# Counting products of the rank passes: four column tiles, in the middle of an LSTM step

## The reference

```python
def step(carry, x_t):
    h_prev, c_prev = carry
    combined = jnp.concatenate((x_t, h_prev), axis=1)
    f_t = jax.nn.sigmoid(combined @ W_f + b_f)
    i_t = jax.nn.sigmoid(combined @ W_i + b_i)
    c_tilde = jnp.tanh(combined @ W_c + b_c)
    c_t = f_t * c_prev + i_t * c_tilde
    o_t = jax.nn.sigmoid(combined @ W_o + b_o)
    h_t = o_t * jnp.tanh(c_t)
    return ((h_t, c_t), h_t)
_, hs = jax.lax.scan(step, (h0, c0), jnp.swapaxes(x, 0, 1))
```

## Time and profile before

| | |
|---|---|
| median of 3 runs | 4644.66 us (4644.18 to 4644.81) |
| the profiled execution's own time | 4646.08 us |
| its span, first to last instruction | 4644.3 us |
| mean granted TensorE clock | 0.971 |
| TensorE matmuls busy | 4446.2 us (96%) |
| VectorE busy | 2307.4 us (50%) |
| ScalarE busy | 1912.3 us (41%) |
| matmuls of line 1007 (the adds), busy | 2310.0 us |
| matmuls of line 1063 (the counting products) | 640 |

### The profile page before, as it was taken

One profiled execution on the slowest core, in us unless ns is written; L12 is line 12 of the kernel. 1 busy time (PEld: TensorE's weight loads), 2 busy tenths in 40 slices (PEclk: granted clock), 3 DMA queues, 4 the chain that ended last, 5 costly groups with the idle time before them and its releaser, 6 DMA issues.

```text
span 4644.3 us, 136942 instructions
## 1 busy us (share of the span) xinstructions
PE 4446.2 (96%) x53052; PEld 2196.5 (47%) x53052; DVE 2307.4 (50%) x10628; ACT 1912.3 (41%) x7133; POOL 361.0 (8%) x351
## 2 busy tenths in 40 slices
PE   9888898999999999999999999999999998799999
PEld 7444554444444444444444444344446745555554
DVE  6424313666666666666666666566632524511111
ACT  0010111566666555666666555455531502111111
POOL 0000001000000222000000232013210001000000
PEclk9998899999999999999999999999999999799999
DMA  2000101620000000000000000000003302011111
GB/s 72 25 34 23 49 28 73 189 85 0 9 0 0 1 2 3 3 0 0 0 0 0 2 2 5 0 1 2 1 26 89 77 32 71 30 46 64 55 64 38
DMA packets 49646, 139.42 MB, mean 30 GB/s; under 512 B 25496, under 2 KB 33455, under 8 KB 38171
## 3 DMA queue, kind: packets, MB, share of 16 engines
q1 hardware_dynamic: 39325, 113.73, 7.5%
q0 software_dynamic: 10208, 24.08, 2.6%
HBM read 114.92 MB, written 22.60 MB: 30 GB/s over the span
## 4 chain that ended last, share of the span: by engine, by line
PE 93%; DVE 5%; ACT 1%; issue 1%; POOL 0%; DVEq 0%; ACTq 0%; POOLq 0%
PE PS L1007 48%; PE PS L724 32%; PE PS L1001 4%; PE PS L1063 3%; PE PS L810 2%; PE PS L1141 1%; PE PS L755 1%; PE PS L1191 1%; PE PS L1131 1%; PE PS L1121 1%; ACT BUF L1286 1%; DVE stats L1588 0%; PE PS L783 0%; DVE BUF L1684 0%; POOL BUF L599 0%
## 5 line engine op out<-in xcount | busy, mean ns | idle before, releaser
L1007 PE MATMUL PS<-BUF,ls_hid 128*1 128x256 f32 x40000 | 2310.0, 380 | 4.8 <-DVE ls_hid L2013 4.7
L1007 PEld LDWEIGHTS PS<-BUF,ls_hid 128*1 128x1 f32 x40000 | 927.3, 84 | 1182.4 <-DVE ls_hid L2013 209.8
L1983 DVE STREAM_TRANSPOSE ls_turn<-PS 128x192 f32<-128x192 f32 x1250 | 478.4, 383 | 547.1 <-PE PS L1007 547.0
L1405 ACT ACTIVATE ls_th<-ls_pr 128x1 f32<-128x1 f32 x2500 | 600.8, 287 | 100.9
L724 PE MATMUL PS<-ring,BUF 128*125 128x512 f32 (+1 forms) x1440 | 619.4, 589 | 23.2 <-DVE BUF L1729 5.8
L724 PE MATMUL PS<-BUF,ring 128*128 128x512 f32 (+1 forms) x2176 | 597.2, 436 | 2.3 <-ACT BUF L1286 1.4
L724 PEld LDWEIGHTS PS<-BUF,ring 128*128 128x128 f32 x2176 | 331.7, 192 | 274.3 <-issue 272.3
L2013 DVE SCALAR_TENSOR_TENSOR ls_hid<-ls_gate,ls_th 128x1 f32<-128x1 f32 x2500 | 345.1, 149 | 233.6 <-ACT ls_th L1405 214.4
L724 PEld LDWEIGHTS PS<-ring,BUF 128*125 128x125 f32 x1440 | 270.6, 190 | 353.2 <-issue 333.4
L1398 ACT ACTIVATE ls_gate<-ls_turn 128x6 f32<-128x6 f32 x1250 | 265.5, 212 | 320.4 <-DVE ls_turn L1983 240.7
L1294 ACT ACTIVATE BUF<-PS,cols 128x625 f32<-128x625 f32 x130 | 101.4, 782 | 625.6 <-PE PS L724 622.7
(11 more groups left out here) (312 smaller groups left out, 3092.8 us busy)
## 6 DMA issues: line engine op xcount, KB each, us to landing
cell_bias<-BUF SPq DMA_DIRECT2D x5, 2441.4 KB
BUF<-cell_bias POOLq DMA_DIRECT2D x5, 2441.4 KB, 15.0
ring<-in_L_wo SPq DMA_DIRECT2D x11, 1024.0 KB, 4.9
ring<-in_L_wi SPq DMA_DIRECT2D x8, 1024.0 KB, 4.9
ring<-in_L_wg SPq DMA_DIRECT2D x8, 1024.0 KB, 4.8
ring<-in_L_wout SPq DMA_DIRECT2D x8, 1024.0 KB, 4.8
gate_inputs<-BUF SPq DMA_DIRECT2D x5, 1344.0 KB
BUF<-in_L_wh SPq DMA_DIRECT2D x4, 1024.0 KB, 12.8
```

Source lines behind the costliest of these rows:

```text
L1007: ins = nc.tensor.matmul(ls_sum[u][f][32 * q:32 * q + 1, :].rearrange("p (j n) -> p j n", j=4), ls_hid[:, c:c + 1], ls_half[:, q, c, :, f, :],
L1405: nc.scalar.activation(ls_th[:, f, c:c + 1], ls_pr[:, f, c:c + 1], ACT.Tanh, scale=0.5, bias=ls_pr[:, f, 2 + c:3 + c]).then_inc(ls_tanh[f], 1)
L1983: V.transpose(ls_turn[:, f, 2:8, :], ls_sum[u][f][:, 64:256].rearrange("p (g n) -> p g n", g=6)).then_inc(ls_turned[f], 1)
```

## The change

Two edits. First, a counting product is no longer one matmul of 125 columns, but four of 32, 32, 32 and 29 columns, each with its output at the partitions 0, 32, 64 and 96, for each of the two ranges of 512 and 113; the same placing as the seeds and adds have. Second, the product is issued in the middle of the step, between `add(0, 1)` and the wait for column 2 of h, and no longer behind the step. With it goes its own wait, on `rk_hot` or `rk_pos`. ScalarE's and VectorE's streams are as they were.

```diff
-                def step(t, u, g):
+                def step(t, u, g, between=None):
...
                     add(1, 0)
                     pe.wait_ge(ls_h[0], t * 2 + 2)
                     add(0, 1)
+                    if between:
+                        between()
                     pe.wait_ge(ls_h[1], t * 2 + 1)
                     add(0, 2)
...
                     for a, b in ((0, 512), (512, N)):
-                        ins = nc.tensor.matmul(PS[0:EP, 1, a:b], m, hot_rank[u][:, a:b], start=False, stop=False,
-                                               skip_group_check=True)
+                        for p in range(0, EP, 32):
+                            e = min(p + 32, EP)
+                            ins = nc.tensor.matmul(PS[p:e, 1, a:b], m[:, p:e], hot_rank[u][:, a:b], start=False, stop=False,
+                                                   skip_group_check=True)
                     return ins
...
                                 chunk = ET * k + (lo - t0) // 2 + u + 1
-                                for v in range(2):
-                                    step(it * 4 + (lo + 2 * u + v), v, g)
-                                    if v == 0:
-                                        pe.wait_ge(rk_hot, it * 2 + chunk)
-                                        rank_add(tri, u).then_inc(rk_cum, 1)
-                                    else:
-                                        pe.wait_ge(rk_pos, it * 2 + chunk)
-                                        rank_add(rest, u).then_inc(rk_all, 1)
+
+                                def count_own():
+                                    pe.wait_ge(rk_hot, it * 2 + chunk)
+                                    rank_add(tri, u).then_inc(rk_cum, 1)
+
+                                def count_rest():
+                                    pe.wait_ge(rk_pos, it * 2 + chunk)
+                                    rank_add(rest, u).then_inc(rk_all, 1)
+                                step(it * 4 + (lo + 2 * u), 0, g, count_own)
+                                step(it * 4 + (lo + 2 * u + 1), 1, g, count_rest)
```

## The result

The changed kernel takes 4976.2 us (median of 4 runs, 4975.44 to 4977.58), the kernel before 4644.46 us. The ratio is 1.0715, with a 95% interval of 1.0696 to 1.0733. It is 7% slower, by 332 us.

A forecast was written before the change was run, and what follows sets the result against it. TensorE was taken to bound the kernel, 93% of the chain. Waits for late operands add 158 x 1.125 + 160 x 0.945 = 329 us to 4646.1, and the median's 1.4 us less gives 4974 us, range 4930 to 5060.

The forecast's parts named there:

- The operand comes after the place: Mid-step product waits for its operand: ready at 2.47 us (own step) or 2.29 (rest), while the gap is at 1.30.
- The product takes 0.27 us: Tiled counting product on TensorE: four tiles abreast at the seeds' rate, 0.27 us for 625 columns.
- What follows takes 2.52 us: From the first add of column 2 to the next step's first add: a latency chain of 2.52 us after the product.
- The steps: Counting steps: own 5.31 us, rest 5.13, against 4.185; 158 and 160 of them add 329 us.
- The first, operands there in time: Rival: operand ready at the mid-step place, step 4.09 us, 30 us faster, 4614 us; chance 5%.
- The tiles do go abreast: Rival claimed the opposite: product's four tiles run one after the other, 1.07 us, 256 us more, 5230 us; chance 4%.
- TensorE's granted clock: Rival: new idle time lowers TensorE's clock in the passes; every second step falling adds 448 us, 5422 us; chance 5%.
- an idle time of 1.0 to 1.2 us: Sign: new TensorE idle time of 1.0 to 1.2 us ahead of the counting product, some 160 of each kind.
- half 0's way to h: Behind the product: half 0's sums through VectorE and ScalarE to h, within the 2.52 us, TensorE's other work in its shadow.
- the sum of 0.51: TensorE cost of an untiled counting product: 0.41 us itself plus seeds taking 0.32 instead of 0.22, together 0.51.
- the first own step of each pass free: First own step of a pass pays no wait, its matrix being made before the pass; so 158 own steps counted.
- More than that the change can't win: Upper bound on gain: counting lengthens a step by 0.30 us (4.19 against 3.89), 96 us over 320 steps.

The follow-up runs named there:

- A step later: Changed kernel with each tiled product kept mid-step but put into the step after its own, where its operand has long been ready: 4622.31 us.
- the run behind add (0, 3): Changed kernel with the tiled products in their own step but 16 adds later, behind the add that completes half 0: 4710.85 us.
- middle, own product alone: Changed kernel with the own product still in the middle of its step, the rest product moved back behind its step: 4780.08 us.

## Why the prediction was right

The forecast was 4974 us, in a range of 4930 to 5060. The measured 4976.2 is the likeliest case, by its own steps.

- **The operand comes after the place.** Forecast at 2.52 us into an own step, with the 0.05 of the release; measured 2.51. For a rest step 2.34 was forecast, and its timeline has 1310.57 - 1308.21 = 2.36. "A step later" shows it from the other side: same place, same matmuls, operand ready, 354 us less.
- **The product takes 0.27 us.** Measured 1305.69 - 1305.42 = 0.27. By the Trainium skill's ratio for three column tiles ("TensorE: Matmul & The Clock Gate", section "Measured speedup vs the span model") I had estimated 0.34. The trace doesn't agree with that estimate for four tiles: one after the other they would have taken 1.07 us, and 0.27 is what the seeds' rate gave for four abreast.
- **What follows takes 2.52 us.** Measured 1308.21 - 1305.69 = 2.52.
- **The steps.** 5.31 was forecast for an own step and 5.30 measured, 5.13 for a rest step and 5.15 measured; the mean of the second pass is 5.23 where the sum has 5.22. 329 us were forecast, and 332 measured.
- **The rivals.** The first, operands there in time, was priced at 4614 us. It isn't this kernel, but it is "a step later", 4622. The tiles do go abreast. And TensorE's granted clock stayed at 1.00 through the first pass of the changed kernel, and through the second (the columns are those of the earlier trace rows):

```profile
868.90:1708.00 839.10, 687.36 (x12884) 276.21 (x12880) 436.80 (x2502) 455.52 (x1771) 2.36 (x3) 1.00 0.09 28
```

That is the upper level, 2.4 GHz, with a wait of about 1 us in every step, while the earlier trace rows show it lower behind idle times of 3.16 us and of 1.86 and 0.65.

Four statements were loose. I forecast an idle time of 1.0 to 1.2 us; the rows give 1.03 and 0.87 for matmuls, since a matmul's end is modelled well behind its start, and 1.54 and 1.38 for weight loads. And I called half 0's way to h the chain that the adds of half 1 lie in the shadow of. That holds for the changed kernel, where the wait comes ahead of both halves. It doesn't hold for a product put between them, as the run behind add (0, 3) showed.

I also put the 0.10 us that the untiled form costs beside its 0.41 into the seeds behind it, after the earlier trace rows; it lies ahead of the product, as the run with the tiles alone shows, and the sum of 0.51 is the same. And I called the first own step of each pass free. It is in the first pass, where the product at 865.76 us waits for nothing. In the second, ScalarE makes both wide activations within that step, and TensorE's matmuls wait 1.31 us for the second of them, which makes this one step 5.58 us long. That is 5.58 - 4.185 = 1.4 us of the 332.

"More than that the change can't win", I wrote of 96 us. The tiles by themselves win 79 of it. With the product behind the step, bare work of 3.68 us and 0.27 for the product make 3.95, and h's own loop would allow 3.89. Of all places that were tried, the old one is the best for the tiled product.

| place of the tiled product | step, us | time, us |
|---|---|---|
| behind the step | 3.95 | 4566 |
| middle, a step later | 4.08 | 4622 |
| behind add (1, 1) | 4.15 | 4636 |
| behind add (0, 3) | 4.45 (own), 4.28 (rest) | 4711 |
| middle, own product alone | 5.18 (own), 4.01 (rest) | 4780 |
| middle (the change) | 5.30 (own), 5.15 (rest) | 4976 |

## What to carry to other kernels

An instruction that is moved takes its wait along, and on an in-order engine everything behind it waits too. Before filling a gap, find in the trace the end of the operation that signals the operand, and count it from the same event as the gap: here the gap was at 1.30 us into the step and the operand at 2.5, behind the very h whose arrival ended the gap. The slack of 1.5 us that the operand had at its old place was what the old place was for.

In a loop that goes through several engines, look for the place where the engine's stream has nothing close behind it that another engine waits for; of the places tried here that was the best. In the middle, filler work lengthens each loop that passes it, and there can be more than one. When an edit has two parts, price them apart: here one was worth 1.7% and the other cost 8%.

## What the runs showed of the hardware

- Eight bf16 matmuls, 125 rows by 32 (or 29) columns on four column tiles, against 512 and 113 columns, take 0.27 us from the first start to the next group's. Two matmuls of 125 columns over the same data take 0.41, and between groups of one-column tiles another 0.10 passes ahead of them (the adds before them take 3.56 instead of 3.46). So an untiled product between tiled groups costs 0.24 us more here than a tiled one, 77 us over 320 steps. How much of the 0.14 behind its start is the change of form and how much its own weight loads, no run separates.
- ScalarE starts the next activation before the one before it is over: the wide activation began 0.11 us after `keep`, which takes 0.21. I had counted 0.42 us for making the matrix first and got 0.51 (1.03 - 0.52); I had let it start only at the end of the last tanh, and it started 0.09 us ahead of that end (1302.07 + 0.48 against 1302.46). The Trainium skill ("ScalarE: Activation LUTs", section "What ACT_TABLE_LOAD costs") gives about 0.093 us for the overlap of activations back to back; the trace agrees, 0.21 - 0.11 = 0.10 us.
